# Attention and FFN layer on one Trainium2 core: first chunk prepared tile by tile, weight turns moved between products, GpSimd adding a negated mean

## What is computed

```python
n = layernorm(x)                       # (x - mean) / sqrt(var + 1e-5), per token
q, k, v = n @ Wq.T, n @ Wk.T, n @ Wv.T # 512, 128 and 128 columns
# 8 heads of 16 in k and v, 4 query groups share them; softmax over all 2048 keys
a_dot = softmax(q @ k.T / 4) @ v
a_mem = elu(q) @ memory / (elu(q) @ memory_norm)
x = x + a_dot * (1 - w) + a_mem * w    # w = sigmoid(memory_weight)
y = layernorm(x)
out = x + fp8_round(y / input_scale) * input_scale @ (weight * weight_scale).T
```

## Time and profile before

| what | us |
|---|---|
| median of 3 runs (lowest, highest) | 2020.57 (2020.05, 2024.47) |
| profiled execution, its own time | 2019.41 |
| span of the profiled execution | 2017.6 |
| TensorE busy in the span | 2000.8 (99%) |
| ScalarE busy | 1937.0 (96%) |
| VectorE busy | 1116.0 (55%) |
| GpSimd busy | 132.1 (7%) |

### The profile page before, as it was taken

The page is one execution under the profiler, slowest core; times in us unless marked ns, Lnnn a source line. Parts: engine busy times, 40 slices in busy tenths (PEclk is TensorE's granted clock), DMA queues, the critical chain, the costliest instruction groups (busy, mean ns, idle before and its releaser), DMA issues.

```text
span 2017.6 us, 63258 instructions
## 1 busy us (share of the span) xinstructions
PE 2000.8 (99%) x27820; PEld 907.9 (45%) x27828; DVE 1116.0 (55%) x1733; ACT 1937.0 (96%) x2191; POOL 132.1 (7%) x164
## 2 busy tenths in 40 slices
PE   8999999999999999999999999999999999999998
PEld 7876533344444444444444444444444444444445
DVE  7786544555455545554555445554555455554555
ACT  5667999999999999999999999999999999999997
POOL 5761000000000000000000000000000000000000
PEclk9999999999999999999999999999999999999999
DMA  6755111121111211121111211121112212221111
GB/s 198 256 198 181 49 49 37 40 52 52 36 41 50 72 46 37 52 72 48 31 48 51 73 38 44 52 73 40 37 49 52 72 31 52 52 72 32 45 50 47
DMA packets 132471, 131.67 MB, mean 65 GB/s; under 512 B 28387, under 2 KB 107643, under 8 KB 132219
## 3 DMA queue, kind: packets, MB, share of 16 engines
q1 hardware_dynamic: 131355, 126.24, 22.3%
q10 hardware_dynamic: 864, 1.57, 0.2%
HBM read 86.57 MB, written 37.49 MB: 61 GB/s over the span
## 4 chain that ended last, share of the span: by engine, by line
PE 93%; DVE 3%; DMA 2%; ACT 1%; issue 1%; POOL 0%; SPq 0%; ACTq 0%; DVEq 0%; POOLq 0%
PE ps L935 43%; PE ps L997 43%; PE ps L821 2%; DMA resid<-in_x 2%; PE ps L1037 1%; PE ps L1021 1%; DVE stats L1164 1%; PE ps L1090 1%; PE ps L1107 1%; DVE ps L1321 0%; DVE y_out L1309 0%; DVE parts L1229 0%; ACT parts L671 0%; PE ps L794 0%; PE ps L775 0%
## 5 line engine op out<-in xcount | busy, mean ns | idle before, releaser
L754 ACT ACTIVATE pool<-ps 128x1024 f32<-128x1024 f32 x1953 | 1795.1, 1164 | 3.7 <-PEq L973 0.8
L935 PE MATMUL ps<-q_st,k_st 99*32 99x512 bf16 x16128 | 1100.5, 378 | 0.7 <-issue 0.4
L997 PE MATMUL ps<-pool,v_st 128*32 128x512 f32 (+1 forms) x8568 | 1061.6, 567 | 0.0
L935 PEld LDWEIGHTS ps<-q_st,k_st 99*32 99x32 bf16 x16128 | 438.2, 95 | 812.5 <-issue 498.2
L997 PEld LDWEIGHTS ps<-pool,v_st 128*32 128x32 f32 x8568 | 270.0, 110 | 210.8 <-issue 0.6
L1450 DVE STREAM_TRANSPOSE by_token<-ps 128x512 f32<-128x512 f32 x63 | 45.2, 717 | 476.6 <-PE ps L997 476.6
L1443 DVE SCALAR_TENSOR_TENSOR late<-late 128x1024 f32<-128x1024 f32 x189 | 231.5, 1225 | 6.5
L1429 DVE TENSOR_SCALAR late<-ps 128x512 f32<-128x512 f32 x126 | 87.1, 691 | 127.2 <-PE ps L935 127.2
L631 POOL TENSOR_TENSOR var_eps<-moments,eps 128x1 f32<-128x1 f32 x32 | 6.1, 190 | 1810.5 <-DVE moments L1479 1810.5
L1506 DVE SCALAR_TENSOR_TENSOR y_out<-ps,scalars,resid 128x512 f32 (+1 forms) x28 | 21.0, 751 | 112.2 <-PE ps L1021 112.2
L1434 DVE SCALAR_TENSOR_TENSOR late<-late 128x1024 f32<-128x1024 f32 x63 | 77.2, 1225 | 2.1
(11 more groups left out here) (150 smaller groups left out, 1001.4 us busy)
## 6 DMA issues: line engine op xcount, KB each, us to landing
v_st<-v_aug SPq DMA_DIRECT2D x64, 256.0 KB
q_aug<-parts SPq DMA_DIRECT2D x32, 384.0 KB, 3.3
q_st<-q_aug SPq DMA_DIRECT2D x64, 192.0 KB
k_st<-k_aug SPq DMA_DIRECT2D x64, 192.0 KB
k_st<-k_aug SPq DMA_DIRECT2D x192, 64.0 KB
sigma_kept<-y_out SPq DMA_DIRECT2D x32, 256.0 KB, 3.7
q_st<-q_aug SPq DMA_DIRECT2D x64, 128.0 KB
wqT<-sigma_kept SPq DMA_DIRECT2D x32, 256.0 KB, 5.2
```

What stands on the lines that cost most here:

```text
L754: act.activation(held[:, half_u * 2 * CH:half_u * 2 * CH + 2 * CH], sc[unit % SLOTS].rearrange("p a b -> p (a b)"), ACT.Exp, scale=EXP_UNIT)\
L935: last = pe.matmul(dst[VW * c:VW * c + VW, :], k_st[0:AUG, par, keys:keys + VW], q_st[0:AUG, par, q * CH:q * CH + CH], start=True, stop=True)
L997: last = pe.matmul(acc[par][VW * c:VW * c + VW, :].rearrange("v (i s) -> v i s", s=VW)[:, places, :], v_st[:, par, j, :], by_place[:, c, p ...
```

## The change

- Chunk 0 goes tile by tile. VectorE takes statistics and moments of one tile, then of the next; GpSimd makes the reciprocal deviation of each tile on its own (an add and a power of one column instead of four); VectorE normalises tile by tile after all moments; TensorE turns a tile as soon as it is normalised.
- TensorE turns tiles 0 and 1 of x, then block 0 of Wq, tiles 2 and 3, and block 1. Block 2 is turned inside strip 0, between the products with `x_high` and those with `x_low`, block 3 after strip 0, Wk and Wv after strip 1. ScalarE's copies and VectorE's splits move accordingly.
- VectorE's moments of chunk 1 move from ahead of strip 0's parts to behind them, and the split of Wq's block 3 stands behind these.
- From chunk 1 on VectorE also writes the negated mean, four numbers a partition, as a further instruction after waiting for its own moments; GpSimd's `normalise` then adds it where it subtracted the mean. GpSimd does all four tiles of chunk 1; VectorE's two go away.
- GpSimd's last settings of constants (`v_tiles`, `ones_row`) move behind the reciprocal deviations of chunk 0.
- SyncE waits for tile 1 of x, no longer tile 0, ahead of the other weight loads.
- `WARM_UP_TURNS` goes from 20 to 16, in both places.

```diff
--- before.py
+++ after.py
@@ -44,7 +44,7 @@
 SIXTEEN_FREE = 16
-WARM_UP_TURNS = 20
+WARM_UP_TURNS = 16
@@ -170,6 +170,7 @@
         rstd = sb("rstd", [P, 2, TPC], F32)
+        minus_mean = sb("minus_mean", [P, 2, TPC], F32)
         rstd_s = sb("rstd_s", [P, TPC], F32)
@@ -271,7 +272,7 @@
         xn_ready = sem("xn_ready")
-        xn_rest_ready = sem("xn_rest_ready")
+        centre_ready = sem("centre_ready")
         tp_ready = sem("tp_ready")
@@ -362,7 +363,7 @@
-            sp.wait_ge(x_tile_loaded[0], 16)
+            sp.wait_ge(x_tile_loaded[1], 16)
             for a in range(KT // 2, KT):
@@ -565,27 +566,39 @@
             pool_e.memset(eps[:, :], LN_EPS).then_inc(consts_set, 1)
+            pool_e.wait_ge(consts_set, 6)
...
+            def rstd_of_tile(t):
+                pool_e.wait_ge(moments_ready, t + 1)
+                pool_e.tensor_tensor(var_eps[:, t:t + 1], moments[:, 0, t:t + 1, 1], eps[:, t:t + 1], ALU.add).then_inc(eps_added, 1)
+                pool_e.wait_ge(eps_added, t + 1)
+                pool_e.tensor_tensor(rstd[:, 0, t:t + 1], var_eps[:, t:t + 1], minus_half[:, t:t + 1], ALU.pow)\
+                    .then_inc(rstd_ready, 1)
...
+            for t in range(TPC):
+                rstd_of_tile(t)
             pool_e.memset(v_tiles[:, :, :, :, DH:VW], 0.0).then_inc(zeros_set, 1)
...
             pool_e.memset(ones_row[:, :], 1.0).then_inc(ones_set, 1)
-            pool_e.wait_ge(consts_set, 6)
             pool_e.wait_ge(ones_set, 2)
             def rstd_of(c, par):
-                pool_e.wait_ge(moments_ready, c + 1)
+                pool_e.wait_ge(moments_ready, TPC + c)
+                pool_e.wait_ge(rstd_ready, TPC + c - 1)
                 pool_e.tensor_tensor(var_eps[:, :], moments[:, par, :, 1], eps[:, :], ALU.add)\
                     .then_inc(eps_added, 1)
-                pool_e.wait_ge(eps_added, c + 1)
+                pool_e.wait_ge(eps_added, TPC + c)
                 pool_e.tensor_tensor(rstd[:, par, :], var_eps[:, :], minus_half[:, :], ALU.pow).then_inc(rstd_ready, 1)
             def normalise(c, par, tiles=TPC):
-                pool_e.wait_ge(rstd_ready, c + 1)
+                pool_e.wait_ge(rstd_ready, TPC + c)
+                pool_e.wait_ge(centre_ready, c)
                 pool_e.wait_ge(tp_ready, c * KT)
                 for t in range(tiles):
-                    last = pool_e.tensor_scalar(xn[:, t, :], resid[:, c * TPC + t, :], moments[:, par, t, 0:1],
-                                                rstd[:, par, t:t + 1], ALU.subtract, ALU.mult)
+                    last = pool_e.tensor_scalar(xn[:, t, :], resid[:, c * TPC + t, :], minus_mean[:, par, t:t + 1],
+                                                rstd[:, par, t:t + 1], ALU.add, ALU.mult)
                 last.then_inc(xn_ready, 1)
@@ -616,10 +629,8 @@
-            rstd_of(0, 0)
-            pool_e.wait_ge(rstd_ready, 1)
             rstd_of(1, 1)
-            normalise(1, 1, TPC // 2)
+            normalise(1, 1)
             for c in range(NG):
@@ -655,9 +666,6 @@
-            for j in range(KT):
-                copy_weight(j)
@@ -707,12 +715,14 @@
                         second_part(c, o - 1)
-                    elif c == 0:
+                    if c == 0 and o == 0:
+                        copy_weight(KT - 1)
+                    elif c == 0 and o == 1:
                         for j in (KT, KT + 1):
...
                         act.activation(e_neg, mem_w, ACT.Exp, scale=-1.0).then_inc(e_neg_ready, 1)
-                    else:
+                    elif o == 0:
                         copy_v(c - 1, 1 - par)
@@ -739,7 +749,10 @@
+            copy_weight(0)
             copy_x_high(0, 0, range(KT))
+            copy_weight(1)
+            copy_weight(2)
             for c in range(NG - 1):
@@ -780,16 +793,17 @@
-            for j in range(KT):
-                turn_weight(j)
+            def turn_first_tile(t):
+                pe.wait_ge(xn_ready, t + 1)
+                for k in range(KT):
+                    last = pe.transpose(turn_bank(0, k)[:, t * P:t * P + P], xn[:, t, k * P:k * P + P], ident[:, :])
+                    if t == TPC - 1:
+                        last.then_inc(tp_ready, 1)
             def turn_xn(c, ks):
-                pe.wait_ge(xn_ready, c + 1)
-                if c == 1:
-                    pe.wait_ge(xn_rest_ready, 1)
+                pe.wait_ge(xn_ready, TPC + c)
                 for k in ks:
-                    if c > 0:
-                        pe.wait_ge(x_low_ready, c * KT + max(k - 1, 0))
+                    pe.wait_ge(x_low_ready, c * KT + max(k - 1, 0))
                     for t in range(TPC):
@@ -845,6 +859,8 @@
                         product(c, par, 0, k, p)
+                if c == 0:
+                    turn_weight(2)
                 for k in range(KT):
@@ -871,13 +887,14 @@
                         project(c, par, o)
-                    if o == 0:
-                        if c == 0:
-                            for j in (KT, KT + 1):
-                                turn_weight(j)
-                        else:
-                            key_norms(c - 1)
-                            turn_v(c - 1)
+                    if c == 0 and o == 0:
+                        turn_weight(KT - 1)
+                    elif c == 0 and o == 1:
+                        for j in (KT, KT + 1):
+                            turn_weight(j)
+                    elif o == 0:
+                        key_norms(c - 1)
+                        turn_v(c - 1)
                     if first_guard and o == 2:
@@ -924,7 +941,12 @@
-            turn_xn(0, range(KT))
+            turn_first_tile(0)
+            turn_first_tile(1)
+            turn_weight(0)
+            for t in range(2, TPC):
+                turn_first_tile(t)
+            turn_weight(1)
             for c in range(NG - 1):
@@ -1159,23 +1181,26 @@
                 for t in range(TPC):
-                    if c == 0:
-                        dve.wait_ge(x_tile_loaded[t], 16)
                     last = dve.bn_stats(stats[:, t, :], resid[:, bass.ds(c * TPC + t, 1), :].rearrange("p a d -> p (a d)"))
-            def mean_and_variance(par):
+            def mean_and_variance(c, par):
                 for t in range(TPC):
...
-            def normalise(c, tiles, done):
-                dve.wait_ge(rstd_ready, c + 1)
-                dve.wait_ge(tp_ready, c * KT)
-                for t in tiles:
-                    last = dve.tensor_scalar(xn[:, t, :], resid[:, c * TPC + t, :], moments[:, c, t, 0:1], rstd[:, c, t:t + 1],
-                                             ALU.subtract, ALU.mult)
-                last.then_inc(done, 1)
+                dve.wait_ge(moments_ready, TPC + c)
+                dve.tensor_scalar(minus_mean[:, par, :], moments[:, par, :, 0], -1.0, None, ALU.mult).then_inc(centre_ready, 1)
...
+            def moments_of_tile(t):
+                dve.wait_ge(x_tile_loaded[t], 16)
+                dve.bn_stats(stats[:, t, :], resid[:, t, :]).then_inc(stats_ready, 1)
+                dve.wait_ge(stats_ready, t + 1)
+                dve.bn_aggr(moments[:, 0, t, :], stats[:, t, :]).then_inc(moments_ready, 1)
...
+            def normalise_tile(t):
+                dve.wait_ge(rstd_ready, t + 1)
+                dve.tensor_scalar(xn[:, t, :], resid[:, t, :], moments[:, 0, t, 0:1], rstd[:, 0, t:t + 1],
+                                  ALU.subtract, ALU.mult).then_inc(xn_ready, 1)
@@ -1194,22 +1219,15 @@
-            statistics(0)
-            dve.wait_ge(stats_ready, 1)
-            mean_and_variance(0)
+            for t in range(TPC):
+                moments_of_tile(t)
+            for t in range(TPC):
+                normalise_tile(t)
             split_weight(0)
-            normalise(0, range(TPC), xn_ready)
+            for k in range(KT):
+                split_x(0, 0, k)
             split_weight(1)
-            for k in range(KT // 2):
-                split_x(0, 0, k)
             split_weight(2)
-            split_x(0, 0, 2)
-            split_weight(3)
-            split_x(0, 0, 3)
-            dve.wait_ge(x_loaded[1], 16)
-            statistics(1)
-            dve.wait_ge(stats_ready, 2)
-            mean_and_variance(1)
             def weights_of_memory():
@@ -1323,8 +1341,8 @@
                 statistics(c)
-                dve.wait_ge(stats_ready, c + 1)
-                mean_and_variance(par)
+                dve.wait_ge(stats_ready, TPC + c)
+                mean_and_variance(c, par)
@@ -1348,9 +1366,14 @@
                     if c == 0 and o == 0:
+                        dve.wait_ge(x_loaded[1], 16)
+                        statistics(1)
+                        dve.wait_ge(stats_ready, TPC + 1)
+                        mean_and_variance(1, 1)
+                        split_weight(KT - 1)
+                    if c == 0 and o == 1:
                         for j in (KT, KT + 1):
                             split_weight(j)
```

(1 more changed line is left out.)

## The result

| | before | after |
|---|---|---|
| median, us (lowest to highest, runs) | 2020.58 (2019.37 to 2024.47, 22) | 2024.62 (2022.24 to 2027.46, 22) |
| ratio to before, 95% interval | | 1.0019 [1.0014, 1.0025] |
| profiled execution, its span | 2019.41, 2017.6 | 2023.6, 2021.9 |
| turn of x behind TensorE's last wait on the loop, starts at | 131.12 | 133.83 |
| GpSimd busy | 132.1 | 102.5 |

The change makes the kernel slower by 4.0 us, 0.2%. The interval of the ratio excludes no change, and the time lies above the range of the prediction (2018.3 to 2023.0).

The account below looks back on a forecast made before the run. The loop of load, VectorE and ScalarE was taken to bound the preparation until 131.12 us: starting 0.65 earlier, plus 0.75 for five negated means, gives +0.1, so 2019.5 us (median 2020.7); 8 in 10 within 2018.3 to 2023.0.

Parts of the forecast that it names:

- `first_part`: Strip 0's first part in chunk 0: forecast at 14.5 us, before 17.63, so 3.1 us won.
- S: The time VectorE begins the moments of chunk 1: forecast 17.5 us against 16.95 before.
- the last part of strip 2: VectorE's part that opens the loop of loads: forecast at 32.4 us, so the loop starts 0.65 us earlier.
- F: GpSimd's time per normalised tile with add: 1.04 us taken, between 0.5 and 2.08; up to 1.2 it costs nothing.
- The wait for `xn`: TensorE's new wait at 24.2 us, ahead of chunk 1's turns: 1.8 us of its 2.3 us lead.
- `k_mean_sq`: TensorE's wait for VectorE in chunk 4: forecast to grow from 1.42 to near 2.0 us.
- The tail: Idle turns end 0.45 us sooner, gap grows from 0.57 to 1.0; no cost taken, at worst 1.4 us.
- I take 0.15: Price in us of each VectorE negated mean: two in chunk 0's stretch, five on the loop; bounds 0.1 and 0.3.
- the turn at 131.12: TensorE's turn after the loop: forecast +0.1 us; a move over 1.5 us either way would show the forecast wrong.
- Rival 1: GpSimd keeps 2.08 us a tile, so chunk 1's turns come late: slower, 2022.5 us; chance 0.2.
- Rival 2: TensorE's slow pace of turns at the start lasts longer, loop 1.2 us later: 2021.9 us; chance 0.12.
- Rival 3: TensorE alone sets the preparation, so its 2.3 us lead at chunk 1 reaches the end: 2018.3 us; chance 0.13.

Follow-up runs that it names:

- The negated mean behind the square: The changed kernel with its new tile allocated last and, from chunk 2 on, VectorE's negation behind `add_sigma` and `rest` of the next strip: 2021.70 us (before 2020.28).
- the two pairs of medians: Changed kernel, VectorE against GpSimd negating: first pair, tile allocated last, 2024.04 against 2020.24 us; second, 32 bytes ahead of the operands, 2024.62 against 2021.95.
- the new start alone: The changed kernel without negated mean or new tile, GpSimd subtracting and chunk 1's tiles split with VectorE as before: 2022.28 us (before 2020.38).
- the first experiment: The changed kernel with the new tile `minus_mean` allocated behind all others, so every other tile keeps its address of before: 2024.04 us (before 2020.28).
- the add alone: The kernel before with VectorE's negated mean and GpSimd's add, old start, chunk 1's tiles still split, new tile allocated last: 2025.12 us (before 2020.28).

## Why the prediction was wrong

**Right: the frame.** The first product (11.1 forecast, 10.63 measured), `first_part` (14.5; 14.15), S (17.5; 17.14) and the last part of strip 2 (32.4; 32.70) came within half a microsecond, and the gain of three microseconds at the start did vanish in VectorE's full stretch, as written. The last of the four was partly luck: S came 0.36 us early and the stretch behind it, 15.56 us for a forecast 14.9, ran 0.66 long. Without its negated means the forecast's stretch is 14.6, and so it is in the kernels where GpSimd negates (14.60 and 14.61): the other terms of that sum were right. F was below its threshold of 1.2 us (0.78 against 1.04 taken). The wait for `xn` was 0.8 us where I had put 1.8; the rest went to waits for VectorE's parts and to a longer one for `x_high` (1.14 instead of 0.65), which is the same lead lost at other doors. `k_mean_sq` was waited for 1.65 us (2.0). The tail has 1.01 us of gap as forecast, and its last turn and products took 0.40 and 1.04 as in the earlier trace rows.

**Wrong: "I take 0.15", five rounds of it 0.75 us.** This is the step that failed. Seven negated means were 1.05 us in the sum and measure 2.7. In the plain rounds the term is 0.24, inside the bounds of 0.1 to 0.3: the instruction is 0.17, and it begins 0.03 us behind the moments. Against before the fifth round has 0.87 more (0.78 against the kernel where GpSimd negates), and the two of chunk 0's stretch cost 0.95 where 0.3 was put. So the turn at 131.12 moved by 2.7 us, past the 1.5 that I had named as the sign of being wrong; 1.25 us of that is the long x load. My upper bound was the length of one small instruction and its wait, taken from rows in which GpSimd was in other work; I never asked which GpSimd instruction would run beside each of the seven, nor which of VectorE's other small instructions would be pushed beside one. A warning was there to be read, in the timeline of the kernel before:

```profile
124.74 1.04 POOL L614 TENSOR_TENSOR q_sq<-parts 128x512 bf16<-128x512 bf16 x1 [0.50 <-ACT parts L671]
124.86 0.16 DVE L1290 CAST guard_bf<-guard_rest 128x1 bf16<-128x1 f32 x1
125.05 0.74 DVE L1292 TENSOR_TENSOR guard_bf<-guard_rest,guard_bf 128x1 bf16<-128x1 f32 x1
```

One element a partition takes 0.74 us beside the square and ends with it, and the cast ahead of it takes 0.16: it does not happen to every instruction. The negated mean behind the square (0.16), the negation on GpSimd (rounds of 12.1) and the two pairs of medians (3.8 and 2.7 us) show the term. Why the first pair has 1.1 us more than the second is open.

The Trainium skill's "GPSIMD Engine Reference", section "Key points", says that GpSimd shares its memory interfaces with VectorE, with contention for VectorE instructions in a two-port mode or with two inputs in SBUF. The trace agrees in that some VectorE instructions stretch beside GpSimd (0.17 to 0.82, 0.99 to 2.00 us) and others do not (the cast, 0.16); no run here separates its conditions.

**Wrong by omission: no term for addresses.** I read the new tile as a name. About 1.2 us of the loss comes with its 32 bytes by the medians, 0.6 of it seen in the profiles. "From 131.12 on TensorE's own work sets the pace, and a shift there passes through" held; that the pace there stays the same did not.

**Wrong in the size of the noise.** The sum said of 4 us that it "is about what a measurement of this kernel can tell from no change"; with 22 runs of each kernel the interval is 1.1 us on either side. "A median that can fall 1 us either way" was no error of size: the profiled execution stood 1.0 us under the changed kernel's median, before's 1.2. Where the mean granted clock of a run reads 1.000, the runs of before have medians of 2019.9, 2020.1, 2019.6 and 2020.5 on the four calls, where it reads lower 2021.7, 2021.4, 2020.3 and 2021.3; of its 110 runs there 51 are of the second kind. Of the changed kernel's 22 runs 13 are, with 2024.8 against 2024.1. So falls of the clock go with slower runs of both kernels, and with the full clock alone they are still some 4 us apart (2024.1 against 2019.6 to 2020.5). That they follow the waits at `k_mean_sq` and `xn` is seen in two profiles only.

**The rivals.** Rival 1 (GpSimd keeps its pace) did not occur, but its mechanism is real: the new start alone ran into it, with a wait of 2.70 us, and took 2022.3 where the rival was priced at 2022.5. That the numbers agree is chance, for in this kernel VectorE normalises two of the four tiles and nobody negates. Rival 2 did not occur: the 16 idle turns took 3.68 us, 0.23 apart, and the eight turns from 7.43 on 1.11 us, 0.14 each, in spite of the pause. The rule cited there left the moment open, and it came earlier than the 8.85 us that I carried over. Rival 3 did not occur either. None of them named what did: a new instruction on the engine of the loop, beside another engine's.

**The sum, redone.** The new start with the fast add and GpSimd negating -0.1 (2020.24 against 2020.38), addresses 1.2, negated means 2.7 by the profiles (2.7 and 3.8 by the medians): 3.8, against 4.0 measured. The first two terms come from medians that are each uncertain by a microsecond or more, so the agreement is no test.

**What stays open.** Why 32 bytes slow the products and 64 half as much (two offsets were tried, and the records don't show a cause), and whether the attention loses by it; why the pair of 3.8 us is above the 2.7 that the other shows: the fall of the clock in the profile of the first experiment (1.5 us) isn't enough, since in runs with a mean clock of 1.000 the two pairs still differ by 3.9 and 2.2 us; whether the long x load of 8.70 us (8.51 in the new start alone, 8.55 in the new start with GpSimd negating and the 32 bytes) has to do with the change: such a load is seen in three of the eight profiles with the new start and in none of the six with the old. VectorE's negation at yet other places, and starts of the allocation other than two, were not tried.

## What to carry to other kernels

Before pricing a small instruction added to a full engine, list what the neighbouring engines do at that moment in every round, and what the small instructions behind it will meet; here one collision of 0.65 us on the chain and 0.5 us of shifted ones cost more together than four plain rounds (0.96). Price it by the chain's length with and without it, too, and not by its own row. Put such an instruction on the engine that has time and on which nobody waits: the same negation cost up to 3.8 us on VectorE and nothing measurable on GpSimd. And allocate a new small tile behind everything else, or try it alone first, so that it moves no operand.

## What the runs showed of the hardware that was not expected

- GpSimd's operation decides its time: subtract and multiply over 128x512 float32 2084 ns, add and multiply 776 ns, the same shapes and operand kinds.
- A VectorE `tensor_scalar` of 128x4 takes 0.17 us alone and 0.82 beside a GpSimd `tensor_tensor`, with which it ends; two of 128x512 take 0.99 us beside GpSimd's subtraction and 2.00 beside its add and squares.
- 32 bytes more ahead of the operands bring products of 397 ns instead of 389, 0.233 us apart instead of 0.2285, and by the medians about 1.2 us over the kernel; 64 bytes bring 393 ns, 0.2305 us and no loss in the median. By the sizes of the tiles, if each is rounded up to 32 bytes, x_high starts 32 past a multiple of 64 before and at a multiple with the 32 bytes; no record shows the addresses.
- TensorE's granted clock fell to 0.50, the level of 1.2 GHz, for some three microseconds in all, falling and rising, behind waits of 2.08 and 2.70 us. In all other profiles it stayed at 1.00 from 8 us to the end of the preparation, behind waits of up to 1.9 us and, in the add alone, one of 2.1.
